# Summing attention probabilities in the later batches on DVE and PE alone

## The reference

```python
q = _qdq(layernorm(x)) @ _qdq(wq).T + bq          # 16 heads of 32
k, v = split(ctx @ wkv.T + bkv)
attn = softmax(einsum('bnhd,bmhd->bhnm', q, k) / sqrt(32))
o = einsum('bhnm,bmhd->bnhd', attn, v)
x = x + tanh(g_xattn) * (_qdq(o) @ _qdq(wp).T + bp)
h = layernorm(x)                                   # weights rounded to fp8
x = x + tanh(g_ffn) * (((silu(h @ gate * gs) * (h @ up * us)) @ down) * ds)
```

## Time and profile before

| | us |
|---|---|
| runs shown | 1009.93, 1011.36 (median), 1013.87 |
| the profiled execution | 1011.81 |
| its span in the profile | 1010.0 |
| busy PE, DVE, ACT, POOL | 885.5, 728.5, 554.4, 397.2 |
| mean granted TensorE clock | 0.944 of full |

### The profile page before, as it was taken

How to read it: one execution, slowest core, us unless ns; L and a number is a source line. 1 busy time by engine, 2 the same in 40 slices (tenths; PEclk the granted TensorE clock), 3 DMA queues, 4 the chain that set the end, 5 groups by cost and what they waited for, 6 DMA issues and landing times.

```text
span 1010.0 us, 13421 instructions
## 1 busy us (share of the span) xinstructions
PE 885.5 (88%) x4872; PEld 312.4 (31%) x4880; DVE 728.5 (72%) x1274; ACT 554.4 (55%) x693; POOL 397.2 (39%) x284
## 2 busy tenths in 40 slices
PE   5978888998999988879999988879899998874898
PEld 2421211144333311135333311125333321122443
DVE  6888969657677779977667779978666778766322
ACT  4547776643565576733566476752556567651230
POOL 1145888720176164540057154470012144470130
PEclk9998999999999998889999988889999998876799
DMA  9234344300211432000211331000200132100001
GB/s 323 76 95 122 102 110 125 104 1 18 51 32 48 123 82 48 1 1 2 50 39 44 106 98 44 21 1 1 47 1 1 37 103 51 37 1 0 1 1 42
DMA packets 37106, 55.27 MB, mean 55 GB/s; under 512 B 8944, under 2 KB 15152, under 8 KB 37040
## 3 DMA queue, kind: packets, MB, share of 16 engines
q1 hardware_dynamic: 35120, 48.13, 16.7%
q0 software_dynamic: 1920, 6.29, 2.2%
HBM read 31.21 MB, written 4.19 MB: 35 GB/s over the span
## 4 chain that ended last, share of the span: by engine, by line
PE 55%; DVE 23%; ACT 10%; issue 8%; POOL 3%; DMA 1%; DVEq 0%; ACTq 0%; POOLq 0%
PE ps L1294 31%; DVE acc L1061 13%; PE ps L1623 8%; ACT r L815 5%; PE ps L1415 4%; PE ps L1436 4%; PE ps L1453 3%; POOL acc L671 2%; PE ps L1477 2%; PE ps L1278 1%; DVE am L917 1%; PE ps L1467 1%; DVE r L1037 1%; ACT r L843 1%; DVE r L1193 1%
## 5 line engine op out<-in xcount | busy, mean ns | idle before, releaser
L815 ACT ACTIVATE r<-ps 128x1024 f32<-128x1024 f32 x256 | 251.6, 1023 | 114.6 <-PE ps L1436 77.7
L671 POOL TENSOR_TENSOR acc<-r,acc 128x1024 f32<-128x1024 f32 x48 | 141.3, 2943 | 177.2 <-ACT r L815 172.6
L1061 DVE TENSOR_TENSOR acc<-acc,r 128x1024 f32<-128x1024 f32 x90 | 179.5, 2016 | 17.9 <-POOL acc L671 9.6
L1436 PE MATMUL ps<-qst,kst 97*128 97x512 f16 x512 | 150.8, 407 | 26.4 <-ACT r L815 25.0
L1453 PE MATMUL ps<-r,vv 128*32 128x512 f32 x1024 | 146.7, 647 | 19.0 <-ACT r L815 14.4
L1037 DVE CUSTOM_DVE_ANT_0 kst<-ps,kst 128x512 f32<-128x512 f32 x192 | 124.5, 686 | 34.5 <-PE ps L1415 32.9
L773 ACT ACTIVATE kst<-ps 128x1024 f32<-128x1024 f32 x96 | 98.2, 1022 | 56.4 <-PE ps L1350 56.1
L689 POOL TENSOR_TENSOR r<-xq,r 128x512 f16<-128x512 f32 x48 | 57.3, 1193 | 145.8 <-ACT r L868 145.4
L1294 PE MATMUL ps<-xs,w_gate 128*128 128x512 f16 x384 | 92.6, 385 | 1.5 <-DVE xs L1225 1.5
L1436 PEld LDWEIGHTS ps<-qst,kst 97*128 97x128 f16 x512 | 37.8, 100 | 181.2 <-ACT r L815 128.9
L1294 PE MATMUL ps<-xs,w_up 128*128 128x512 f16 x384 | 91.2, 380 | 0.0
(11 more groups left out here) (149 smaller groups left out, 1308.2 us busy)
## 6 DMA issues: line engine op xcount, KB each, us to landing
kst<-k_reg SPq DMA_DIRECT2D x192, 64.0 KB
qst<-q_reg SPq DMA_DIRECT2D x192, 32.0 KB
xs<-in_x SPq DMA_DIRECT2D x4, 1024.0 KB, 5.9
cf<-in_ctxT POOLq DMA_DIRECT2D x16, 256.0 KB, 3.4
xres<-in_x SPq DMA_DIRECT2D x4, 1024.0 KB, 5.3
out<-xres SPq DMA_DIRECT2D x16, 256.0 KB, 2.0
acc<-in_down_w SPq DMA_DIRECT2D x10, 256.0 KB, 2.6
vv<-in_wkvT SPq DMA_DIRECT2D x2, 1024.0 KB, 9.9
```

The costliest lines, as they stand in the source:

```text
L671: nc.gpsimd.tensor_tensor(sums, prob[:, p:p + 2, :], sums, ALU.add).then_inc(p_pool, 1)
L815: nc.scalar.activation(prob[:, s:s + 2, :], ps[:, first_bank:first_bank + 2, :], ACT.Exp, scale=SCALE).then_inc(exp_done, 1)
L1061: nc.vector.tensor_tensor(sums, other, prob[:, p:p + 2, :], ALU.add).then_inc(p_dve, 1)
L1436: mm = nc.tensor.matmul(bank(first_bank + k), kst[0:97, g % 2, j + k, t * P:(t + 1) * P], qst[0:97, g % 2, j + k, :], start=True, stop=True)
```

## The change

In batches 1 to 3 DVE now adds 26 of the 32 units, both halves, in order; the table is replaced by `ADDED`. PE sums the other six (units 7, 11, 15, 19, 23, 31). POOL adds nothing; its power step and `residual_bias` now stand at the start of the batch's list. `totals` moves from t = 1 to t = 0. The sums of unit 7 are now the first product into the bank of the denominators. ACT's copy of a group's output waits for the values alone. The first batch is unchanged.

```diff
--- before
+++ after
-ADDS = {}
-for _g in range(G):
-    _last = 7 if _g < G - 1 else 6
-    ADDS[_g, 0] = [("DVE", (0, 1))] + [("DVE", (t,)) for t in range(2, _last + 1)]
-    ADDS[_g, 1] = [("DVE", (0, 1))] + [("POOL" if t < 6 else "DVE", (t,)) for t in range(2, _last + 1)]
...
+ADDED = ((0, 1, 2, 3, 4, 5, 6), (0, 1, 2, 4, 5, 6), (0, 1, 2, 4, 5, 6), (0, 1, 2, 3, 4, 5, 6))
+ADD_HEADS = 2
+ADD_PARTS = HG // ADD_HEADS
+ADD_UNITS = [g * MT + t for g in range(G) for t in ADDED[g][1:]]
 def added(b, u):
-    return b > 0 and (u, 0) in ADD_OF
+    return b > 0 and u % MT in ADDED[u // MT]
-def add_count(b, index):
-    e, n = index
-    return (b - 1) * len(ADD_ORDER[e]) + n + 1
+def add_count(b, u, j):
+    at = u + 1 if u % MT == 0 else u
+    return ((b - 1) * len(ADD_UNITS) + ADD_UNITS.index(at)) * ADD_PARTS + j // ADD_HEADS + 1
@@ POOL
-            def add_units(b):
-                for n, (u, h, g, k) in enumerate(ADD_ORDER["POOL"]):
-                    pool.wait_ge(exp_done, pair_count(b, u, 2 * h))
-                    by, m = ADD_INDEX[g, h, k - 1]
-                    pool.wait_ge({"POOL": p_pool, "DVE": p_dve}[by], add_count(b, (by, m)))
...
-                    nc.gpsimd.tensor_tensor(sums, prob[:, p:p + 2, :], sums, ALU.add).then_inc(p_pool, 1)
-                    if n == 1 and b < B - 1:
-                        inverse_deviation(variance_of_x(b + 1))
-                residual_bias(b)
             for b in range(B):
                 if b == 0:
                     first_units()
                 else:
-                    add_units(b)
+                    if b < B - 1:
+                        inverse_deviation(variance_of_x(b + 1))
+                    residual_bias(b)
                 inverse_deviation(variance_of_x2(b))
@@ ACT, exponentials
                         if freed >= 0 and added(b, freed):
-                            index = ADD_OF[freed, j // 2]
-                            act.wait_ge({"POOL": p_pool, "DVE": p_dve}[index[0]], add_count(b, index))
+                            act.wait_ge(p_dve, add_count(b, freed, j + 1))
...
                     if t == 0 and g > 0:
-                        if added(b, u - 1):
-                            act.wait_ge(p_used, b * UNITS + u)
-                        else:
-                            act.wait_ge(o_full, g)
+                        act.wait_ge(o_full, b * G + g)
                         nc.scalar.copy(oT[:, g - 1, :], bank(O_BANK)).then_inc(o_out, 1)
@@ DVE (replaces the loop over ADD_ORDER["DVE"])
+            def add_unit(b, u):
+                if u not in ADD_UNITS:
+                    return
+                g = u // MT
+                first = u % MT == ADDED[g][1]
+                if first and g > 0:
+                    dve.wait_ge(acc_read, (b - 1) * (G - 1) + g)
+                elif first:
+                    dve.wait_ge(x_done, b * NT)
+                    dve.wait_ge(ctx_ready, min(b + 1, B - 1) * CHUNKS)
+                for j in range(0, HG, ADD_HEADS):
+                    sums, p = acc[:, j:j + ADD_HEADS, :], p_slot(b, u, j)
+                    dve.wait_ge(exp_done, pair_count(b, u, j + ADD_HEADS - 1))
+                    if first:
+                        q = p_slot(b, u - 1, j)
+                        other = prob[:, q:q + ADD_HEADS, :]
+                    else:
+                        other = sums
+                        dve.wait_ge(p_dve, add_count(b, ADD_UNITS[ADD_UNITS.index(u) - 1], j))
+                    nc.vector.tensor_tensor(sums, other, prob[:, p:p + ADD_HEADS, :], ALU.add).then_inc(p_dve, 1)
@@ PE, sums
-                                          ..., start=(u == 0), stop=(u == UNITS - 1))
+                                          ..., start=(u == (MT - 1 if b else 0)), stop=(u == UNITS - 1))
@@ PE, totals
-                for h in range(2):
-                    index = ADD_INDEX[g, h, len(ADDS[g, h]) - 1]
-                    pe.wait_ge({"POOL": p_pool, "DVE": p_dve}[index[0]], add_count(b, index))
+                pe.wait_ge(p_dve, add_count(b, g * MT + ADDED[g][-1], HG - 1))
...
-                                          start=(g == 0), stop=False)
+                                          start=False, stop=False)
@@ PE, loop over units
-                    if b > 0 and t == 1 and g > 0:
+                    if b > 0 and t == 0 and g > 0:
                         totals(b, g - 1)
```

More of the change, by code:

```diff
@@ L412, in build @@
         s_full, exp_done, p_used = sem("s_full"), sem("exp_done"), sem("p_used")
-        p_pool, p_dve, acc_read = sem("p_pool"), sem("p_dve"), sem("acc_read")
+        p_dve, acc_read = sem("p_dve"), sem("acc_read")
         o_full, o_out, den_out = sem("o_full"), sem("o_out"), sem("den_out")
@@ L661, in first_units @@
                 residual_bias(0)
-            def add_units(b):
-                for n, (u, h, g, k) in enumerate(ADD_ORDER["POOL"]):
-                    pool.wait_ge(exp_done, pair_count(b, u, 2 * h))
-                    by, m = ADD_INDEX[g, h, k - 1]
-                    pool.wait_ge({"POOL": p_pool, "DVE": p_dve}[by], add_count(b, (by, m)))
-                    sums = acc[:, 2 * h:2 * h + 2, :]
-                    p = p_slot(b, u, 2 * h)
-                    nc.gpsimd.tensor_tensor(sums, prob[:, p:p + 2, :], sums, ALU.add).then_inc(p_pool, 1)
-                    if n == 1 and b < B - 1:
-                        inverse_deviation(variance_of_x(b + 1))
-                residual_bias(b)
             for b in range(B):
@@ L1040, in maxima @@
                     ins.then_inc(m_free, 1)
[L1042 to L1051, removed]
-                        other = sums
-                    else:
-                        if g > 0:
-                            dve.wait_ge(acc_read, (b - 1) * (G - 1) + g)
-                        else:
-                            dve.wait_ge(x_done, b * NT)
-                            dve.wait_ge(ctx_ready, min(b + 1, B - 1) * CHUNKS)
-                        q = p_slot(b, u - 1, 2 * h)
-                        other = prob[:, q:q + 2, :]
-                    nc.vector.tensor_tensor(sums, other, prob[:, p:p + 2, :], ALU.add).then_inc(p_dve, 1)
+            def add_unit(b, u):
[15 more added lines that the diff above has]
+                    else:
+                        other = sums
+                        dve.wait_ge(p_dve, add_count(b, ADD_UNITS[ADD_UNITS.index(u) - 1], j))
+                    nc.vector.tensor_tensor(sums, other, prob[:, p:p + ADD_HEADS, :], ALU.add).then_inc(p_dve, 1)
             dve.wait_ge(split_hi, CT)
@@ L1168, in _ @@
                     else:
-                        add_units(b, u)
+                        add_unit(b, u)
                     for _ in range(W_UNITS[u] if b == 0 else 0):
@@ L1467, in sums @@
                     mm = nc.tensor.matmul(ps[j * DH:(j + 1) * DH, DEN_BANK, :], esel[:, g, :],
-                                          prob[:, p_slot(b, u, j), :], start=(u == 0), stop=(u == UNITS - 1))
+                                          prob[:, p_slot(b, u, j), :], start=(u == (MT - 1 if b else 0)), stop=(u == UNITS - 1))
                 mm.then_inc(p_used, 1)
             def totals(b, g):
-                for h in range(2):
-                    index = ADD_INDEX[g, h, len(ADDS[g, h]) - 1]
-                    pe.wait_ge({"POOL": p_pool, "DVE": p_dve}[index[0]], add_count(b, index))
+                pe.wait_ge(p_dve, add_count(b, g * MT + ADDED[g][-1], HG - 1))
                 for j in range(HG):
                     mm = nc.tensor.matmul(ps[j * DH:(j + 1) * DH, DEN_BANK, :], esel[:, g, :], acc[:, j, :],
-                                          start=(g == 0), stop=False)
+                                          start=False, stop=False)
                 if g < G - 1:
```

## The result

The changed kernel takes 951.6 us (median of four runs, 948.18 to 953.38) against 1011.54: a ratio of 0.940, interval 0.937 to 0.944. That is faster by 60 us, where 48 were forecast, and inside the range of 946 to 985. A second set of runs gave 951.78 and 0.942 (0.940 to 0.944).

What follows compares the result with a forecast made beforehand. No engine was full: DVE's and POOL's adds hindered each other, stalling PE and lowering its clock, with ACT waiting some 30 us per batch. Gains of 17.0 + 17.0 + 14.4 = 48.4 from 1011.81 gave 963.4 us, range 946 to 985.

Steps and rivals of the forecast that it cites:

- rival A: First group's adds are not late, since DVE could run ahead where units wait: 947 us; chance 0.14.
- DVE's adds, their price: Per batch, 44 DVE adds at 1.14 us, 50.2 us; with other work at most 67.6, so DVE bounds only locally.
- ACT's idle time: ACT's idle in the window of a batch's units falls from 30 us to about 14.
- PE's sums: Five more units per batch on PE: a lone sum costs 0.9 us, one followed by totals 1.9.
- Batch 1 placed piece by piece: Batch 1: two adds meet residual_bias, first totals at 365.8, clock falls, copy at 423.9 against 440.91; gain 17.0 us.
- 3.02 and 3.29 from there: After the first totals' wait, clock fallen: 3.02 us to the next exponential, 3.29 to the unit after.
- Batch 3: Three of the first group's last adds meet residual_bias, until 834.2; clock falls, unit 10 at 840.5; gain 14.4 us.
- The tail: Behind batch 3's units, part of the rest of the span: carried over, gain 0.
- Batch 2: Batch 2 shows the same busy times as batch 1, so gains 17.0 us again.
- B: DVE late at totals of groups 1 and 2 too, clock falls at every boundary: 22 us more, 985 us; chance 0.15.
- C: Adds slow for another reason than POOL, DVE becomes the bound: 1027 us; chance 0.04.
- D: Stacking DMAs bind: 4 us more would make two waits of 2 per batch, 12 us, 975 us; chance 0.06.

Runs made afterwards that it cites:

- all_dve: Kernel before with POOL's adds given to DVE, no units to PE, POOL's power step and residual_bias at the batch's start: 965.2 us, ratio 0.954.
- pool16: Changed kernel plus 16 more POOL operations of 128 x 512 per batch right after residual_bias: 981.3 us (two runs), ratio 0.971.
- best: end_t1 with units 11 and 19 of batch 3 given back to DVE: 941.5 us, ratio 0.931.
- late: Changed kernel with POOL's residual_bias waiting for DVE's last add of group 0: 945.2 us, ratio 0.936.
- t1: Changed kernel with totals put back to t = 1 of the next group: 945.2 us, ratio 0.935.
- end_t1: Changed kernel with totals at t = 1 and residual_bias after DVE's last add of the batch: 941.9 us, ratio 0.931.
- rep: Changed kernel run again, nothing edited: 951.8 us, ratio 0.942.
- serial: Changed kernel with each DVE add also waiting for the DVE add just before it: 975.0 us, ratio 0.964.
- pool_stays: Kernel before with six units per batch on PE and totals at t = 0, POOL's adds kept: 986.1 us, ratio 0.976.
- late_t1: Changed kernel with residual_bias after DVE's last add of group 0 and totals at t = 1: 945.0 us, ratio 0.935.
- pow3: Changed kernel with one more POOL power step in batch 3 ahead of residual_bias, after unit 4's adds: 951.5 us (one run).

## Why the prediction was right, and where it was not

The range held. The single figure of 963 did not come so close: 951.6 is nearer to the 947 of rival A. The sum of the three batches and of what was carried over is 10 us short of the gain in the profile, and two steps make most of it, batch 3 and the tail.

*DVE's adds, their price.* Right. 1.14 us each in a run, a mean of 1277 ns in batch 1, and DVE 67.3 us busy there, where 67.6 was the bound. all_dve shows the cause by itself, pool16 in the other direction. One sign was misjudged: ACT's idle time was to fall to about 14 us in the group of its exponentials and fell to 19.4, because a third of the gain lies in front of the last copy, outside that group.

*PE's sums.* Right: 0.89 for a lone sum (0.9), 1.27 and the copy's half microsecond for a sum with totals (1.9). best takes two away and gains 1.7.

*Batch 1 placed piece by piece.* Right to half a microsecond: the totals of group 0 started at 365.98 (365.8), the copy came at 424.13 (423.9). That this lateness is POOL's residual_bias and the order of totals was shown by late, t1 and end_t1, which take batches 1 and 2 from between 76.4 and 79.3 to 73.0. Part of the precision was luck: rep's batch 1 took 2.9 less, with the same collision, the same wait and a clock that did not fall. The term "3.02 and 3.29 from there" is one outcome of several.

*Batch 3.* Wrong. The step "three of the last adds meet residual_bias" failed. The price of a meeting was right (2.31 and 2.28 us in batch 1, 2.29 taken) and the meeting did not take place: DVE's adds of alternating halves leave no gap, and the operation of POOL that arrived in the eighth add of the run was kept out, 5.99 us. With no wait there was also no fall of the clock. 5.1 us of the 10 missed. The row from which I took the meeting did not show an operation that arrives. In the kernel before, the residual operations follow POOL's own adds without a break:

```profile
424.30 9.76 POOL L671 TENSOR_TENSOR acc<-r,acc 128x1024 f32<-128x1024 f32 x3
434.02 6.90 POOL L636 TENSOR_TENSOR xres<-xres,bp_bc 128x512 f32<-128x512 f32 x4
```

So the two engines were already taking turns, and the add of 2.29 us stood right behind another with no gap. I carried this over to a POOL that comes from idle. A wait before each add cannot be the whole difference either: 17 of the 39 adds of over 1.5 us in the later batches of the kernel before follow the instruction ahead of them without idle time. serial shows that gaps let POOL in in batch 3; what decides where there are none is open. Rival A, which I gave 0.14, is what happened in batch 3, and in batches 1 and 2 not.

*The tail.* Wrong by omission: "the rest of the span is carried over". Behind batch 3's units the kernel before took 103.3 us, the changed one 99.95. Windows of the two at the same distances behind the copy (before, then after; the third column from the end is the clock):

```profile
935.00:942.00 7.00, 3.65 (x16) 3.27 (x16) 4.55 (x8) 2.34 (x4) 0.00 (x0) 0.50 0.00 0
942.00:955.00 13.00, 12.94 (x52) 5.57 (x53) 2.15 (x3) 3.08 (x5) 2.26 (x2) 0.86 0.01 1
```

```profile
880.00:887.00 7.00, 5.28 (x24) 4.08 (x25) 2.85 (x5) 2.34 (x4) 0.00 (x0) 0.69 0.00 0
887.00:900.00 13.00, 13.00 (x62) 5.88 (x60) 2.88 (x4) 4.27 (x7) 3.39 (x3) 1.00 0.00 1
```

The clock is 0.69 and 1.00 where it was 0.50 and 0.86. Over all profiles the tail goes with the clock in these two windows: 0.50 and 0.86 in the kernel before and serial (103.3 us), 0.50 and 0.93 or 0.94 in pool_stays, late_t1 and rep (101.7), 0.65 to 0.80 and 1.00 in the others (99.4 to 100.2). In the kernel before, serial and pool_stays PE had waited for the last adds and did their last sums wholly or partly at the slow level. But rep is the changed kernel, entered the chain at the fast level and still took 1.7 us more than its first profile. So of the 3.4 us about half is spread from one execution to the next; that the rest is the wait for the last adds is argued, no run isolates it.

*Batch 2* gained 1.6 more than placed: its clock recovered one product sooner than in batch 1 (unit 10 follows unit 9 by 2.37 us instead of 3.59).

*Rivals B, C, D.* None came. B: no wait for totals in groups 1 to 3, and the clock stayed. C: adds without POOL beside them take 1.2 us. D: the stacking copies never held back a score; in batch 3 the last of them is issued by 828.1, and the scores that need it start at 830.4. The forecast of a gain was safe, since all mechanisms but C had the same sign.

## What to carry to other kernels

Two engines that share something may each be fast and together slow: giving the slower one's work to the faster one can pay even if it then has 40% more to do. When a wait sits in an in-order list, look at what is queued behind it before moving it forward; one unit later cost nothing here and saved 6 us. And a rate of taking turns read from a trace belongs to the situation there: check whether the two engines were already taking turns or one of them arrives from idle, and whether there are gaps between the instructions that it meets.

## What the runs showed of the hardware

A POOL operation from idle that arrived in the eighth or ninth of DVE's back-to-back f32 adds of two SBUF tiles was kept out until the run ended: 5.99, 6.07 and 6.03 us (the changed kernel, rep, t1) for one of 1.26, 7.29 in all_dve, 5.33 for a power step of 1.03 in pow3. A wait of each add for the one before, which makes the distance between their starts 1.36 instead of 1.14 us, ended that (longest 2.26). It is no rule for every arrival: a power step that came 0.24 us into the first add behind a break got in after that add (1.89 instead of 1.03). When the two take turns, a DVE add beside a POOL operation of 1.26 us takes 2.28 to 2.31 instead of 1.22.

The Trainium skill (SBUF — State Buffer, Who interferes with whom) says that the loser blocks fully, for the other's whole instruction. The runs are near that where the two take turns, with 1.06 to 1.09 us lost to an operation of 1.26, and they show the block of POOL to last over several instructions of DVE in the cases above.

After the same wait of 3.4 us for the totals, 21.2 us after the first exponential, PE's clock fell to the lower level in both batches of the changed kernel's first profile and in batch 2 of rep (eight passes in 1.80 to 1.94 us), and stayed at the higher in batch 1 of rep (1.06). The batch took 79.3 us in the one case and 76.4 in the other.
